# One activation over two banks in the attention's shifted-score ring, and a ring of three key tiles for the probabilities

## The reference, cut to what matters

```python
scores = jnp.einsum('bqhd,bkhd->bhqk', q, k)
attn = jax.nn.softmax(scores, axis=-1)
out = jnp.einsum('bhqk,bkhd->bqhd', attn, v).reshape(B, S, D)
```

## Time and profile before

| what | value |
|---|---|
| median of 3 runs | 3162.61 us (3158.49 to 3173.70) |
| profiled execution, its time | 3166.37 us |
| profiled execution, its span | 3164.3 us |
| mean granted TensorE clock | 0.932 |
| PE busy | 2853.7 us, 90% of the span |
| DVE busy | 2438.1 us, 77% |
| ACT busy | 2219.3 us, 70% |
| nested 1, first to last `copy_mix` | 265.03 to 586.13 us |
| nested 2, first to last `copy_mix` | 1452.21 to 1773.32 us |

### The profile page before, as it was taken

How to read it: one execution, slowest core, us unless ns; L and a number is a source line. 1 busy time by engine, 2 the same in 40 slices (tenths; PEclk the granted TensorE clock), 3 DMA queues, 4 the chain that set the end, 5 groups by cost and what they waited for, 6 DMA issues and landing times. The chain is left out here.

```text
span 3164.3 us, 53194 instructions
## 1 busy us (share of the span) xinstructions
PE 2853.7 (90%) x19734; PEld 1646.9 (52%) x19734; DVE 2438.1 (77%) x3759; ACT 2219.3 (70%) x3896; POOL 187.9 (6%) x398
## 2 busy tenths in 40 slices
PE   7869999879999999869999899799997777799999
PEld 4644444423333333343444566688885454578887
DVE  6678999599999999577999354677776677677777
ACT  2357888759999999757888532488885444378887
POOL 0030000300000000020000200100000000010000
PEclk9969999979999999968999899799998888889999
DMA  1043220130100000042220100311110000111111
GB/s 29 1 128 64 42 42 2 33 83 22 22 22 22 22 22 12 7 142 46 42 42 2 29 1 1 78 48 44 48 47 12 1 0 0 54 41 53 53 51 47
DMA packets 76902, 115.24 MB, mean 36 GB/s; under 512 B 13904, under 2 KB 38512, under 8 KB 76656
## 3 DMA queue, kind: packets, MB, share of 16 engines
q1 hardware_dynamic: 76656, 111.99, 14.4%
HBM read 85.73 MB, written 25.43 MB: 35 GB/s over the span
## 5 line engine op out<-in xcount | busy, mean ns | idle before, releaser
L842 DVE TENSOR_REDUCE nested_a_halves<-banks 128x2 f32<-128x1024 f32 x512 | 613.1, 1222 | 74.0 <-PE banks L934 70.8
L889 ACT ACTIVATE nested_a_p<-banks 128x512 f32<-128x512 f32 x1024 | 552.8, 598 | 114.6 <-PE banks L964 90.3
L842 DVE TENSOR_REDUCE wide_a_halves<-banks 128x2 f32<-128x1024 f32 x512 | 593.9, 1218 | 33.3 <-PE banks L934 32.2
L889 ACT ACTIVATE wide_a_p<-banks 128x512 f32<-128x512 f32 x1024 | 554.3, 598 | 45.6 <-PE banks L964 34.2
L1771 DVE TENSOR_TENSOR mix_e_h_low<-mix_e_h,mix_e_h_high 128x512 fp32r<-128x512 f32 x512 | 349.9, 689 | 173.7 <-ACT mix_e_h_high L1877 165.7
L1894 ACT ACTIVATE mix_e_h<-banks,mix_b_folded 128x512 f32<-128x512 f32 x512 | 353.6, 691 | 102.3 <-PE banks L1948 101.8
L977 PE MATMUL banks<-nested_a_p,nested_values 128*32 128x256 f32 x4096 | 328.5, 400 | 0.0
L977 PE MATMUL banks<-wide_a_p,wide_values 128*32 128x256 f32 x4096 | 322.0, 392 | 0.0
L1877 ACT ACTIVATE mix_e_h_high<-mix_e_h 128x512 fp32r<-128x512 f32 x512 | 319.5, 624 | 0.0
L934 PE MATMUL banks<-nested_k_stack,nested_q_stack 48*128 48x512 f32 x1024 | 273.3, 529 | 41.7 <-DMA nested_q_stack<-nested_q_parts 21.9
L964 PE MATMUL banks<-nested_q_stack,nested_k_stack 50*128 50x512 f32 x1024 | 252.6, 423 | 11.1 <-ACT nested_a_p L889 10.3
(11 more groups left out here) (364 smaller groups left out, 4069.8 us busy)
## 6 DMA issues: line engine op xcount, KB each, us to landing
mix_e_gate<-mix_gates_t SPq DMA_DIRECT2D x128, 256.0 KB, 3.1
nested_q_stack<-nested_q_parts SPq DMA_DIRECT2D x96, 128.0 KB
nested_q_parts<-nested_q_cut SPq DMA_DIRECT2D x16, 512.0 KB
nested_k_parts<-nested_k_cut SPq DMA_DIRECT2D x16, 512.0 KB
nested_k_stack<-nested_k_parts SPq DMA_DIRECT2D x32, 256.0 KB
wide_q_stack<-wide_q_parts SPq DMA_DIRECT2D x192, 32.0 KB
nested_k_stack<-nested_k_parts SPq DMA_DIRECT2D x32, 128.0 KB
mix_raw_w<-L_ffn_w_t SPq DMA_DIRECT2D x8, 512.0 KB, 8.1
```

The costliest lines, as they stand in the source:

```text
L842: dve.tensor_reduce(halves[:, half, i, 2 * a:2 * a + 2], bank[:, at:at + 2, :], AX, ALU.max).then_inc(maxed, 1)
L889: act.activation(p[:, kt % 4, j, :], bank[:, ST + n % RING, :], ACT.Exp, scale=scale).then_inc(probs, 1)
```

## The change

In the second pass, items are now counted through the whole stage (item = 32 u + n) and stand in the ring by that count. ACT raises items in threes: the first two, in banks 4 and 5, by one activation of 1024 columns, the third, in bank 6, by one of 512. `raised(item)` is the number of activations up to and with the one that holds the item, and PE's waits on `probs` use it. A pair of items that lie in two key tiles writes across them, so `p` becomes a flat ring of twelve items, three key tiles, where it had four. Each activation waits that the key tile three back has been mixed. `copy_mix` stands behind item 4 in place of item 3. A unit has 32 items, so the threes begin at another place in each of three units that follow each other.

```diff
     ST, MIX = 4, 7
     UNITS = 2 * hd.total
@@ -775,6 +776,13 @@
     def special_place(u):
         return (17 * u + 10) % 2 * 2
+    LAST = UNITS * ITEMS - 1
+    def raised(item):
+        return item // RING * 2 + (2 if item % RING == 2 else 1)
     def slot(u):
@@ -792,7 +800,7 @@
         shift_rows = sb("shift_rows", [8, 2, T2], hd.kind)
         mix = sb("mix", [P, T2])
         inverse = sb("inverse", [P, 4, G])
-        p = sb("p", [P, 4, G, T2])
+        p = sb("p", [P, 3 * G, T2])
         with nc.Block() as block:
@@ -880,14 +888,16 @@
             @block.scalar
             def _(act):
-                def exponential(u, kt, j):
-                    n = 4 * kt + j
-                    act.wait_ge(shifted, u * ITEMS + (n + 1))
-                    if j == 0:
-                        wait_past(act, mixed, u * TILES + (kt - 3))
-                    act.activation(p[:, kt % 4, j, :], bank[:, ST + n % RING, :], ACT.Exp,
-                                   scale=scale).then_inc(probs, 1)
+                def exponential(item):
+                    count = 1 if item % RING == 2 or item == LAST else 2
+                    act.wait_ge(shifted, item + count)
+                    for tile in {item // G, (item + count - 1) // G}:
+                        wait_past(act, mixed, tile - 2)
+                    at = item % (3 * G)
+                    act.activation(p[:, at:at + count, :], bank[:, ST + item % RING:ST + item % RING + count, :],
+                                   ACT.Exp, scale=scale).then_inc(probs, 1)
                 def copy_shifts(u):
@@ -904,13 +914,13 @@
                 copy_shifts(0)
                 for u in range(UNITS):
-                    for kt in range(TILES):
-                        for j in range(G):
-                            exponential(u, kt, j)
-                            if kt == 0 and j == 3 and u:
-                                copy_mix(u - 1)
-                            if kt == 5 and j == 1 and u + 1 < UNITS:
-                                copy_shifts(u + 1)
+                    for n in range(ITEMS):
+                        if (u * ITEMS + n) % RING != 1:
+                            exponential(u * ITEMS + n)
+                        if n == 4 and u:
+                            copy_mix(u - 1)
+                        if n == 21 and u + 1 < UNITS:
+                            copy_shifts(u + 1)
                 copy_mix(UNITS - 1)
             @block.tensor
@@ -958,24 +968,25 @@
                     kt, j = n // 4, n % 4
                     if n == 0:
                         pe.wait_ge(shift_in, (u + 1) * SHIFT_LOADS)
-                    last = n - RING if n >= RING else max(range(n, ITEMS, RING)) - ITEMS
-                    wait_past(pe, probs, u * ITEMS + (last + 1))
+                    item = u * ITEMS + n
+                    if item >= RING:
+                        pe.wait_ge(probs, raised(item - RING))
                     rows, slab = hd.rows_of(j, 2)
-                    pe.matmul(bank[:, ST + n % RING, :], k_stack[rows, slot(u), slab, kt * P:(kt + 1) * P],
+                    pe.matmul(bank[:, ST + item % RING, :], k_stack[rows, slot(u), slab, kt * P:(kt + 1) * P],
                               q_stack[rows, slot(u), slab, u % 2 * T2:(u % 2 + 1) * T2],
                               start=True, stop=True).then_inc(shifted, 1)
                 def mix_values(u, kt, c):
                     if c == 0:
-                        pe.wait_ge(probs, u * ITEMS + kt * G + G)
+                        pe.wait_ge(probs, raised(u * ITEMS + kt * G + G - 1))
                     if kt == 0 and c == 0:
                         wait_past(pe, mix_copied, u)
                     cols = slice(c * P * 2, (c + 1) * P * 2)
                     for j in range(G):
                         last = pe.matmul(bank[32 * j:32 * j + 32, MIX, cols],
-                                         hd.values[:, u // 2, kt, 32 * j:32 * j + 32], p[:, kt % 4, j, cols],
+                                         hd.values[:, u // 2, kt, 32 * j:32 * j + 32], p[:, (u * TILES + kt) % 3 * G + j, cols],
                                          start=(kt == 0 and c == 0), stop=(kt == TILES - 1 and c == 1))
                     if c == 1:
                         last.then_inc(mixed, 1)
```

## The result

| | before | changed |
|---|---|---|
| median of the runs | 3168.15 us (4 runs) | 3368.77 us (4 runs, 3348.36 to 3374.43) |
| ratio, 95% interval | | 1.0615 [1.0578, 1.0653], slower |
| profiled execution | 3166.37 us | 3369.92 us |
| mean granted clock | 0.932 | 0.925 |

The forecast was 3330 us in 3230 to 3410. The kernel is 200 us slower, 203.5 between the two profiled executions, where the sum had 169.

The account below looks back on a forecast made before the run. PE's own work was taken to set the step, with a matmul-Exp-matmul loop just under it. Wide +86, nested +77 and stage ends +6 make +169 on 3166.4: 3335, with the median 3.8 lower 3330 us, range 3230 to 3410.

Parts of the forecast that it names:

- The loop through the pair: Wide ring: matmul, 1.02 us pair activation, next matmul make two gaps of three 1.51 us; units about 22.9 us.
- The gap with the turns: Wide, one gap per unit: 2.19 us before, 2.0 chosen once DVE is early, -0.2 us a unit.
- Worth nothing on ACT: Raising pairs together saves ACT 0.05 us on each of 683 pairs, 36 us in all, but ACT has room.
- Nested, 24.2 us a unit: Nested stages: eight gaps grow from 1.24 to 1.53 us; with smaller terms +2.4 us a unit, +77 us.
- The upper bound: Long gaps might also show nested weight loads (0.18 us) and a 0.06 us hop everywhere: +77 us, 3407.
- The clock at 1.00: Sign expected in the changed kernel's profile: granted clock stays at 1.00.
- Rival 2: PE's pauses lower the clock; a fifth of 1024 steps at 2.09 us adds 140 us: 3470 us, 6%.
- The wait for the DMA of the shift rows, -0.5 a unit: Wide and nested: one gap's existing wait for that DMA is covered by the longer gaps, saving 0.5 us a unit.
- The unit's start: Two gaps behind the copy of the mix: wide 2.19, 2.94, 3.38 us by kind, mean 2.84, +0.2 us; nested +0.2.
- Rival 1: Only one gap of three is long because PE catches up behind it: 3236 us, 12%.
- Rival 3: Faster: ACT's throughput limits each unit's start and the pair's ring waits are hidden; 36 us come off, 3130 us, 5%.
- no change: The gaps just fit and nothing is gained: 3160 us, 2%.

Follow-up runs that it names:

- aligned order: The changed kernel with PE's shifted scores placed by the threes, so no pair lies in two steps: 3204.93 us, 1.0135 of the kernel before.
- singles: The changed kernel with every item raised by its own activation of 512 columns, all else kept: 3110.29 us, 0.9826 of the kernel before.
- singles with late release: The changed kernel with 512-column activations only, but PE waits for both banks of a pair until its second activation ends: 3246.17 us, 1.0247 of the kernel before.

## Why the prediction was right, and where it was off

- **The loop through the pair.** Right, and to the hundredth in wide: activation 1.02 forecast, 1.025 measured; long gap 1.51, measured 1.50 and 1.53; two of three long; unit 22.9, measured 22.92. The single terms hold too: eight of the other twelve gaps are long in each of the three kinds of unit, and the two gaps behind the copy take 2.19, 2.97 and 3.39 us, for 2.19, 2.94 and 3.38. The third of these is here, from 1101.45 to the second item of the last row, which starts at 1104.84:

```profile
1101.45 0.38 PE L975 MATMUL banks<-wide_q_stack,wide_k_stack 50*128 50x512 bf16 x2
...
1102.95 0.39 PE L975 MATMUL banks<-wide_q_stack,wide_k_stack 50*128 50x512 bf16 x2 [0.90 <-ACT wide_a_p L899]
...
1104.33 0.90 PE L975 MATMUL banks<-wide_q_stack,wide_k_stack 50*128 50x512 bf16 x2
```

  The gap with the turns fell further than thought, to 1.9 us and not 2.0, so part of the agreement to the hundredth is luck. The removal of the pairs alone takes 258 us off. The pair's two halves, late release and late start, are 136 and 123 us of it.
- **Worth nothing on ACT.** Right. ACT's busy time fell, from 2219.3 us to 2172.3, and nothing got faster by it. The aligned order shows it once more: with most of the waits gone it still does not beat the singles, nor the kernel before.
- **Nested, 24.2 us a unit.** Measured 24.7. The term that was mis-sized is the long gap of 1.53, taken for both places. The timeline of nested 1:

```profile
405.96 0.40 PE L975 MATMUL banks<-nested_q_stack,nested_k_stack 50*128 50x512 f32 x2
...
406.38 2.67 ACT L899 ACTIVATE nested_a_p<-banks 128x1024 f32<-128x1024 f32 x3 [0.63 <-PE banks L975]
...
407.46 0.19 PEld L975 LDWEIGHTS banks<-nested_q_stack,nested_k_stack 50*128 50x128 f32 x2 [0.42 <-ACT nested_a_p L899]
...
407.46 0.50 PE L975 MATMUL banks<-nested_q_stack,nested_k_stack 50*128 50x512 f32 x2
...
409.11 0.18 PEld L975 LDWEIGHTS banks<-nested_q_stack,nested_k_stack 50*128 50x128 f32 x1 [0.35 <-ACT nested_a_p L899]
...
410.44 0.41 PE L975 MATMUL banks<-nested_q_stack,nested_k_stack 50*128 50x512 f32 x2
```

  The first gap is 1.50, the second 1.65 (407.46 to 409.11), the third 1.33. When PE is released by the wait, its weight load of 0.19 us, else done under the matmul before, comes with the matmul, whose row is 0.50 long in place of 0.40. The next pair's activation, the last of the three that end at 409.05, starts at 408.03, 0.57 after 407.46, where 0.45 was forecast. So a load behind a wait costs some 0.12 us, not its whole length, in one of the two long gaps. The upper bound had such a term; the sum had left it out. Some 14 us over the nested units.
- **The clock at 1.00.** Wrong. Rival 2 had the effect, and the wrong size: 27 us and not 140. It also expected PE to be busy 84% of the time; PE's rows are busy 184 of 200 us in wide and 86 of 90 in nested 1. With the nested term this makes 41 against the 34 missing. The kernel before had a longer spell at the start of nested 2: from the stage's first shifted score to its first copy of the mix it took 35.8 us (1416.4 to 1452.2) and the changed kernel 32.6 (1564.8 to 1597.4), where nested 1 took 29.1 and 31.2. Those 5 us may be most of the rest.
- **The wait for the DMA of the shift rows, -0.5 a unit.** The size was right, the cause wrong. It was PE waiting for item 30, because the old ring began anew in each unit and gave item 0 a bank that had been filled only two items before. The change removes that by counting through, and not by longer gaps that cover it. So the change holds a gain of 36 us, which the prediction had in its sum but did not see as something that can be had without the pairs.
- **The unit's start.** Three kinds of units were forecast and three are there, and their mean fits, in wide to 0.03 us a kind. The same walk gave 0.2 us for the later copy of the mix alone, where its run showed 0.39, so on the whole it is good to some 0.2 us.
- **The other signs.** PE's loads for the shifted scores waited for ACT about nine times a unit in wide, as forecast. DVE's idle time before its maxima is 2.7 us a unit (86.8 in 32), not 3.5.
- **Rival 1** (one long gap of three) falls for the changed kernel; it is what singles with late release do. **Rival 3** and no change fall.

## What to carry to other kernels

Before two buffers of a small ring are consumed by one longer instruction, write down the loop producer - consumer - producer: with three banks the pair's activation was 0.43 us longer than a single one, and it had to wait for both inputs, in a loop that had 0.03 us to spare; an engine's fixed cost of 0.05 us a piece was saved on an engine that nobody waited for. If the merging is wanted, the producer's order has to follow the groups, and then its own cost of splitting pairs has to be counted. And look where a ring starts anew: counting it through the stage was worth 1.1%, moving a copy behind one more piece of work another 0.9%, both for a changed line or three.

## What the runs showed of the hardware that was not expected

- PE paused for only about 0.4 us at a time in most steps, PE's rows are busy 184 of 200 us in wide, and yet the granted clock fell to 1.2 GHz for some 3 to 31 us at a time, mostly at other places in the two traces, and for longer in the nested stages. There PE's rows are busier than in wide: 86 of 90 us.
- A weight load of 0.19 us that is hidden under the matmul before costs some 0.12 us when a wait stands before it (0.57 us from release to ACT in place of 0.45).
- Two matmuls in different rows of the array cost 0.22 us together and 0.22 each when they are placed apart, which made a cycle of the aligned order 3.54 us long where three old steps took 3.33.
